# Narrow cross attention as one program per layer, with packed norm statistics and key and query units inside the batch loop

## The reference, cut to what matters

```python
y_dca, y_main = y[:, -DCA:, :], y[:, :-DCA, :]
kv_dca = (y_dca @ Wkv_dca + bkv_dca).reshape(b, DCA, 2, H, HD)
k_dca = _ln(kv_dca[:, :, 0], kn_dca_w, kn_dca_b);  v_dca = kv_dca[:, :, 1]
q = _ln((x @ Wq + bq).reshape(b, s1, H, HD), qn_w, qn_b)      # norm over 16 features
k = _ln(y_main @ Wk + bk, kn_w, kn_b);  v = y_main @ Wv + bv  # per head, as above
out = (softmax(q k / 4) v + softmax(q k_dca / 4) v_dca) @ Wo + bo
x = x + out                                                   # q is made of layernorm(x)
```

## Time and profile before

| what | us |
|---|---|
| median of 3 runs (lowest, highest) | 3232.19 (3231.69, 3232.72) |
| profiled execution, first to last instruction (the page gives no other time of it) | 3231.0 |
| L1 narrow cross attention, first instruction to the last addition to x | 238.7 |
| the same of L2 and of L3 | 238.2, 240.9 |

### The profile page before, as it was taken

How to read it: one execution, slowest core, us unless ns; L and a number is a source line. 1 busy time by engine, 2 the same in 40 slices (tenths; PEclk the granted TensorE clock), 3 DMA queues, 4 the chain that set the end, 5 groups by cost and what they waited for, 6 DMA issues and landing times. The chain is left out here.

```text
span 3231.0 us, 47747 instructions
## 1 busy us (share of the span) xinstructions
PE 2781.8 (86%) x17648; PEld 1732.3 (54%) x17648; DVE 1936.2 (60%) x2606; ACT 1423.1 (44%) x2574; POOL 917.8 (28%) x774
## 2 busy tenths in 40 slices
PE   7999986899997978789988875667989798998897
PEld 5998953466645647433345522223654455554686
DVE  3555545322268827444468779667965799994442
ACT  3333343121265536322265553446657666652123
POOL 0111100033104513000005400001530799990362
PEclk9999998899998989989998988878999899999898
DMA  4000004111200000200000000000000221213124
GB/s 154 1 0 0 0 7 154 64 46 45 68 29 2 2 21 2 82 1 0 0 20 2 11 4 0 0 20 1 2 28 14 78 77 67 77 44 107 50 87 145
DMA packets 72275, 122.16 MB, mean 38 GB/s; under 512 B 10720, under 2 KB 53088, under 8 KB 71584
## 3 DMA queue, kind: packets, MB, share of 16 engines
q1 hardware_dynamic: 63168, 95.25, 8.9%
q0 software_dynamic: 8928, 24.39, 2.5%
HBM read 100.88 MB, written 18.74 MB: 37 GB/s over the span
## 5 line engine op out<-in xcount | busy, mean ns | idle before, releaser
L3054 POOL TENSOR_TENSOR h<-ssm_u,ss_bc 128x1024 f32<-128x1024 f32 x88 | 205.6, 2358 | 0.0
L3017 ACT ACTIVATE ssm_p_h<-ss_delta,ss_decay 128x256 f32<-128x256 f32 x352 | 146.6, 463 | 123.6 <-DVE ctxT L3091 84.0
L2966 PE MATMUL ssm_p_y<-ctxT,ident 128*128 128x512 f32 x412 | 187.8, 596 | 0.0
L1375 POOL MEMSET ctxT<- 128x512 f32 x3 | 1.6, 526 | 602.8 <-POOLq L60 602.8
L639 POOL TENSOR_TENSOR xw_prob<-xw_prob,xw_rsum 128x512 f32<-128x512 f32 x64 | 65.8, 1039 | 361.1 <-DVE xw_rsum L620 361.1
L3086 DVE TENSOR_TENSOR_SCAN ssm_p_h<-ssm_p_h,h 128x1024 f32<-128x1024 f32 x64 | 145.8, 2279 | 8.5 <-ACT ssm_p_h L3017 6.8
L499 PEld LDWEIGHTS xw_p_q<-xw_u,xw_vo_h 128*128 128x128 f32 x1024 | 116.1, 192 | 10.7 <-ACT xw_u L569 10.2
L3044 POOL TENSOR_TENSOR ctxT<-ctxT,ss_bc 128x1024 f32<-128x1024 f32 x50 | 117.4, 2355 | 15.5 <-DVE ctxT L3084 15.5
L490 PEld LDWEIGHTS xw_p_q<-h,xw_m_h 128*128 128x128 f32 x1024 | 116.8, 192 | 8.9 <-issue 8.9
L2950 PE MATMUL ssm_p_h<-ssm_b_diagonal,ssm_uT 128*128 128x128 f32 x640 | 85.0, 289 | 40.6 <-DVE ctxT L3091 19.6
L2966 PEld LDWEIGHTS ssm_p_y<-ctxT,ident 128*128 128x128 f32 x412 | 76.5, 192 | 79.5 <-issue 78.3
(11 more groups left out here) (747 smaller groups left out, 7188.0 us busy)
## 6 DMA issues: line engine op xcount, KB each, us to landing
ss_bc<-ss_bc_rows SPq DMA_DIRECT2D x24, 896.0 KB, 4.4
ss_bc<-ss_bc_rows SPq DMA_DIRECT2D x8, 768.0 KB, 4.1
L3f_rows<-L3f_rows_out SPq DMA_DIRECT2D x16, 384.0 KB, 3.9
L0f_wg<-in_L_ffn_gate SPq DMA_DIRECT2D x9, 512.0 KB, 10.2
L0f_wu<-in_L_ffn_up SPq DMA_DIRECT2D x9, 512.0 KB, 9.9
L0f_wd<-in_L_ffn_down SPq DMA_DIRECT2D x9, 512.0 KB, 10.2
L0f_rows<-L0f_rows_out SPq DMA_DIRECT2D x16, 256.0 KB, 3.5
x<-in_xT SPq DMA_DIRECT2D x1, 2048.0 KB, 7.5
```

The lines of the kernel that those rows point to most:

```text
L2966: mm = pe.matmul(p_y[:, 2 * half:2 * half + 2, :].rearrange("p e t -> p (e t)"), k.ident[:, :], weighed[n % RING_W][:, ts(half, CH)], star ...
L3017: i = act.activation(out[:, ts(e, CT)], delta[:, e, ts(c, CT)], ACT.Exp, scale=decay[:, E4 * s + e:E4 * s + e + 1])
L3054: g.tensor_tensor(tiles(drive[n % RING]), u[:, c % 2, :, :], bcast(bcs[:, row_b(s), :], 1, E4), ALU.mult).then_inc(sem["driven_g"], 1)
```

## The change

Both programs become one, with one set of semaphores and no barrier. The 16 DCA tokens now lie first in each batch of the context (`SEG = ((DCA, S2), (0, DCA))`, rolled on the host), so `tails` (512 KB load) and the memset of `ctxT` go. The layer norm becomes `PackedNorm`: statistics of the four chunks in 4 x 32 partitions of one PSUM bank (one Ln and one Exp for all), spread again by matmuls into PSUM, where VectorE reads them. The 12 units come in the order `UNITS`; the first four (keys 0 to 2, query 0) are made ahead of the loop, the other eight (query 1, keys 3, 4, query 2, key 5, query 3, keys 6, 7) in the loop, in three pieces, in steps 3j-1, 3j and 3j+1 for j = 0 to 7: piece 0 is `project`, `add_bias` and `squares`; piece 1 is `tally` (head means into 4 x 32 partitions) and `inverse` (Ln and Exp of 128 elements per partition); piece 2 is `widen` (spread by a matmul that carries the norm weight), `multiply` on VectorE (reads PSUM) and `affine` on GpSimd (adds the shift). The squares move from VectorE to ScalarE. Projections and widened factors of the late units use the PSUM tile of the transposes (`p_tw`, `p_t`), the head means that of the values (`p_v`). `values` is one matmul of 512 columns and its copy two; `mix` of batch n-3 now stands ahead of `turn` of batch n-2; the output projection and the addition to x are for two batches each, every second step. The x addition t stands in VectorE's step 2t+5, after the reciprocal. `mix` waits for `added`, since it shares a bank with the output projection. All loops are unrolled. The kernel's start loads one matrix less (`head_mean`).

The diff, cut to what the argument uses ("..." marks what is left out):

```diff
+class PackedNorm:
...
+    def means(self, pe):
+        for a in range(H2):
+            for c in range(NCH):
+                mm = pe.matmul(self.p_stat[self.row(c), :], self.k.mean_ones[:, 0:32], self.src[:, a, ts(c, CH)], start=a == 0, stop=a == H2 - 1, skip_group_check=True)
+        mm.then_inc(self.sem["mean"], 1)
+
+    def copied(self, act):
+        act.wait_ge(self.sem["mean"], 1)
+        act.copy(self.stat[:, 0, :], self.p_stat).then_inc(self.sem["copied"], 1)
+
+    def spread(self, pe, pair):
+        pe.wait_ge(self.s_c, 16)
+        pe.wait_ge(self.sem["copied"], 1)
+        if pair == 1:
+            pe.wait_ge(self.sem["centred"], 2)
+        for c in (2 * pair, 2 * pair + 1):
+            mm = pe.matmul(self.p_wide[:, c % 2, :], self.pick[self.row(c), :], self.stat[self.row(c), 0, :], start=True, stop=True, skip_group_check=True)
+        mm.then_inc(self.sem["spread"], 1)
+
+    def centre(self, v, c):
+        v.wait_ge(self.sem["spread"], c // 2 + 1)
+        v.tensor_tensor(self.dst[:, :, ts(c, CH)], self.src[:, :, ts(c, CH)], bcast(self.p_wide[:, c % 2, :], 1, H2),
+                        ALU.subtract).then_inc(self.sem["centred"], 1)
+
...
+    SEG = ((DCA, S2), (0, DCA))
...
+    UNITS = ((KN, 0), (KN, 1), (KN, 2), (QN, 0), (QN, 1), (KN, 3), (KN, 4), (QN, 2), (KN, 5), (QN, 3), (KN, 6), (KN, 7))
+    EARLY, EVERY = 4, 3
...
+        p_sf = ps(k, ctx, "p_s", [P, 4, CH])
+        p_s = p_sf[:, :, 0:HALF].rearrange("p r (o s) -> p r o s", o=H2)
+        p_tw = ps(k, ctx, "p_t", [P, H2, CH])
+        p_t = p_tw[:, :, :].rearrange("p o (r q) -> p o r q", r=4)
+        p_v = ps(k, ctx, "p_v", [P, CH])
+        p_ys = ps(k, ctx, "p_y", [P, CH])
+        p_y = p_ys[:, 0:D].rearrange("p (o t) -> p o t", o=H2)
+        p_o = p_ys[:, D:D + P].rearrange("p (o t) -> p o t", o=H2)
+        p_c = p_ys[:, 0:3 * H2].rearrange("p (n o) -> p n o", n=3)
+        p_b = p_ys[:, P:P + 2 * H2].rearrange("p (o n) -> p o n", o=H2)
+        ln = PackedNorm(k, ctx, sem, k.x, k.h, p_v[:, :], p_tw, pick, s_c)
...
+        def front(i):
+
+            at = 2 * ((i + 1) % 2)
+            return p_sf[:, at:at + 2, :] if i < EARLY else p_tw
+
+        def variance(i):
+
+            return p_ys[:, 0:P] if i < EARLY else p_v[:, 0:P]
...
+        def at_step(n):
+
+            late = len(UNITS) - EARLY
+            return [(EARLY + j, n + 1 - EVERY * j) for j in range(late) if 0 <= n + 1 - EVERY * j < EVERY]
...
+            def turned_before(n):
+                if n >= 3:
+                    pe.wait_ge(sem["turned_read"], 2 * (n - 2))
+                else:
+                    pe.wait_ge(ln.sem["normed"], NCH)
...
+            def tally(i):
+                pe.wait_ge(s_h, 32)
+                pe.wait_ge(sem["squared"], i + 1)
+                if i >= 1:
+                    pe.wait_ge(sem["logged"], i)
...
+                for part in range(2):
+                    for j in range(4):
+                        at = 2 * P * (j % 2) + P * part
+                        mm = pe.matmul(variance(i)[32 * j:32 * j + 32, :], of_head[:, part, :], square[:, i % 2, j // 2, at:at + P], start=part == 0, stop=part == 1, skip_group_check=True)
+                mm.then_inc(sem["tallied"], 1)
+            def widen(i):
+                kind, _ = UNITS[i]
+                pe.wait_ge(sem["inverse"], i + 1)
+                for at in range(4):
+                    for m, (s0, s1) in kinds(kind):
+                        for o in range(H2):
+                            rows = slice(64 * o, 64 * o + 64)
+                            mm = pe.matmul(front(i)[:, o, at * P + s0:at * P + s1], heads[rows, m, at, :], rv[rows, i % 2, s0:s1], start=True, stop=True, skip_group_check=True)
+                mm.then_inc(sem["widened"], 1)
...
+            def values(n, tallied):
+                if n >= 1:
+                    pe.wait_ge(sem["v_copied"], n)
+                else:
+                    pe.wait_ge(ln.sem["rstd"], 1)
+                    pe.wait_ge(s_o, 32)
+                pe.wait_ge(sem["logged"], tallied)
+                pe.matmul(p_v[:, :], k.ctxT[:, ts(n, S2)], wv[:, :, :].rearrange("p n f -> p (n f)"), start=True, stop=True, skip_group_check=True).then_inc(sem["valued"], 1)
...
+            def mix(n):
+                pe.wait_ge(sem["v_copied"], n + 1)
                 if n >= 1:
-                    pe.wait_ge(sem["v_copied"], n)
+                    pe.wait_ge(sem["mixed_read"], n)
                 if n >= 2:
...
+            def step(n):
+                if 0 <= n < B - 1:
+                    score(n + 1)
+                units = at_step(n)
+                tallied = EARLY
+                for i, part in units:
+                    if part == 1:
+                        if n >= 3:
+                            pe.wait_ge(sem["v_copied"], n - 2)
+                        else:
+                            pe.wait_ge(ln.sem["rstd"], 1)
+                        tally(i)
+                    tallied = i + 1 if part >= 1 else i
+                if within(n, 2, B + 2):
+                    values(n - 2, min(tallied, len(UNITS)) if units else len(UNITS))
+                for i, part in units:
+                    if part == 0:
+                        turned_before(n)
+                        project(i)
+                    elif part == 2:
+                        turned_before(n)
+                        widen(i)
+                if n == -1:
+                    score(0)
+                if within(n, 3, B + 3):
+                    mix(n - 3)
+                if within(n, 2, B + 2):
+                    for i, part in units:
+                        if part == 0:
+                            pe.wait_ge(sem["biased"], i + 1)
+                        elif part == 2:
+                            pe.wait_ge(sem["scaled"], i + 1)
+                    turn(n - 2)
+                if n >= 4 and n % 2 == 0:
+                    project_out((n - 4) // 2)
+
+            ln.means(pe)
+            merge_keys()
+            merge()
+            ln.spread(pe, 0)
+            project(0)
+            ln.spread(pe, 1)
+            project(1)
+            ln.variances(pe, 0)
+            tally(0)
+            ln.variances(pe, 1)
+            widen(0)
+            merge_out()
+            tally(1)
+            ln.spread_inverse(pe, 0)
+            project(2)
+            widen(1)
+            ln.spread_inverse(pe, 1)
+            tally(2)
+            project(3)
+            widen(2)
+            tally(3)
...
+            def step(n):
+                units = at_step(n)
                 if within(n, 0, B):
                     act.wait_ge(sem["shifted"], n + 1)
-                    act.activation(prob[:, u, :, :, :], prob[:, u, :, :, :], ACT.Exp, scale=0.25).then_inc(sem["exped"], 1)
-                if within(n, 1, B + 1):
-                    act.wait_ge(sem["valued"], n)
-                    own = vx[:, (u + 1) % 2, :, :, :].rearrange("p o (r j) (s d) -> p (o r) (j s) d", j=2, s=2)[:, :, 0:4:3, :]
-                    act.copy(own, p_v.rearrange("p (g j d) -> p g j d", j=2, d=HD)).then_inc(sem["v_copied"], 1)
+                    act.activation(prob[:, n % 4, :, :, :], prob[:, n % 4, :, :, :], ACT.Exp, scale=0.25).then_inc(sem["exped"], 1)
+                for i, part in units:
+                    if part == 1:
+                        inverse(i)
                 if within(n, 2, B + 2):
+                    m = n - 2
+                    act.wait_ge(sem["valued"], m + 1)
+                    if m >= 2:
+                        act.wait_ge(sem["mixed"], m - 1)
+                    act.copy(own(m, slice(0, P)), p_v[:, 0:D].rearrange("p (g j d) -> p g j d", j=2, d=HD)).then_inc(sem["v_main"], 1)
+                    act.wait_ge(sem["v_main"], m + 1)
+                    act.copy(own(m, slice(0, DCA)), p_v[0:DCA, D:2 * D].rearrange("p (g j d) -> p g j d", j=2, d=HD)).then_inc(sem["v_copied"], 1)
+                for i, part in units:
+                    if part == 0:
+                        add_bias(i)
+                if within(n, 3, B + 3):
+                    m = n - 3
+                    act.wait_ge(sem["mixed"], m + 1)
+                    if m >= 4:
+                        act.wait_ge(sem["out_proj"], m // 2 - 1)
+                    act.copy(us[:, m // 2 % 2, :, ts(m % 2, S)], p_o).then_inc(sem["mixed_read"], 1)
+                if within(n, 2, B + 2):
+                    m = n - 2
                     for o in range(H2):
-                        act.wait_ge(sem["turned"], 2 * n + o - 3)
+                        act.wait_ge(sem["turned"], 2 * m + o + 1)
+                        if m >= 1:
+                            act.wait_ge(sem["mixed"], m)
                         act.copy(probT[:, o, :, :, :].rearrange("p r j t -> p (r j t)"), p_t[:, o, :, :].rearrange("p r q -> p (r q)")).then_inc(sem["turned_read"], 1)
-                    act.wait_ge(sem["mixed"], n - 1)
```

(123 more changed lines are left out.)

467 lines of the change are left out of this document (204 added, 263 removed).

## The result

The changed kernel takes 3364.86 us (median of 4 runs, 3361.26 to 3366.89) against 3232.11 (4 runs, 3231.69 to 3232.72) before: ratio 1.0407, 95% interval 1.0393 to 1.0421. The forecast was 3325, with 3190 to 3420 as its range: the sign is right, the cost is 133 us where 93 were forecast. The profiled execution's span is 3362.5, 131.5 more than the 3231.0 of before.

What follows compares the result with a forecast made beforehand. VectorE and TensorE bound the loop before; after the change, latency through in-order queues does. 22.6 us more a stage, 68 in three, plus 25 for the clock, makes 93 over the span of 3231.0: 3325 by the median, range 3190 to 3420.

Steps and rivals of the forecast that it cites:

- start to the scores of batch 3: Part of a stage up to batch 3's scores: 94.4 us before, 58.6 after, a gain of 35.8.
- unit stretch, without clock: Batch 3's scores to batch 24's, seven late units as serial chains of waits: 154.9 us, 7.4 a step.
- clock in it: TensorE's clock loss in the steps with units: 1.2 us a unit, 8 a stage, 25 in all.
- seven steps without a unit: Batches 24 to 31, VectorE at 4.03 plus 0.22 us a step: 4.25 each, 29.8 in all.
- after the scores of batch 31: End of a stage: 18.9 us before, one shorter projection at the end, so 18.0.
- stage: One whole narrow cross attention: 238.7 us before, 261.3 after, plus 8 for the clock.
- The rival of pieces that fit: In the loop, late units' pieces fit: some 15 us a unit, 3150 in all; chance 0.17.
- the signs that the forecast named: Unit steps: `multiply` waits near 5 us, `tally` above 1, scores 21 to 23 per three steps, VectorE idle a third.
- `widen` of keys: Spread of a key unit's factors on TensorE: 1.3 us at the scores' pace, taken; 4.2 at the merge's.
- the rival with the clock mostly at half: Clock falls for most unit steps: 5 to 9 us more a unit, 3390 to 3490 in all; chance 0.14.
- the 22.6: Forecast growth of one stage without clock loss, from 238.7 to 261.3 us; 68 in three stages.
- the two additions: VectorE's additions to x in front of multiply 3, ahead of the loop: 2.6 us, done at 39.3.

Runs made afterwards that it cites:

- e6: Changed kernel plus 512-column products nobody reads, on TensorE in its longest wait of each unit (three behind `widen` or two behind the output projection): 3320.69 us.
- e5: Changed kernel plus one VectorE sum over 896 elements per partition (1.09 us) per loop unit, directly ahead of `multiply`: 3363.14 us.
- e1: Changed kernel with `multiply` moved on VectorE behind the sums, the reciprocal and the addition to x of its step: 3293.68 us.
- e2: Changed kernel with ScalarE's order changed: squares ahead of the copies of the transposes, `inverse` ahead of Exp of the batch: 3320.98 us.
- e8: Kernel before with only its second program replaced by the new loop; norm and all twelve units stay in the first program: 3198.54 us, ratio 0.9891.
- e3: Changed kernel with the edits of e1 and e2 together: 3285.63 us.

## Why the prediction was right or wrong

| step of the prediction (us a stage) | forecast | measured |
|---|---|---|
| start to the scores of batch 3 | 58.6 | 68.4 |
| unit stretch, without clock | 154.9 | 155.2 (e6) |
| clock in it | 8 | 11.6 (e6) |
| seven steps without a unit | 29.8 | 29.1 |
| after the scores of batch 31 | 18.0 | 16.5 |
| stage | 269.3 | 280.8 |

**What bounds the loop.** Right. Latency through in-order queues, not busy time, sets the unit stretch: e5 adds work at no cost, e1 and e2 move work and gain 71 and 44. The rival of pieces that fit was to be recognised by unit steps under 6.2; they are 7.9 in the mean (166.8 / 21). Of the signs that the forecast named, these are in the trace: tally's wait for squares above 1 (1.23 in key units), VectorE idle for a third or more, `multiply` waiting for `widen` (6.8 in the mean of the five key units and 4.1 of the three query units, where near 5 was said), scores 4.2 apart after batch 24 where 4.3 was said. Two were missed: scores are 22.7 to 26.2 apart per three steps where 21 to 23 were said, three of the seven above 24, and batch 3's come at 68.4 where 55 to 65 were said.

**The unit stretch.** Right in its sum at full clock, 155.2 (e6) for 154.9, but in part because errors cancel: the first of the seven units, which still starts at half clock, takes 23.1 for 21.2, and five of the others less than was said. `widen` of keys takes 1.96, not 1.3: it lay between the bounds, and the scores' pace, from which 1.3 came, doesn't hold for the small products (16 columns) in it. `tally` takes 0.65, not 0.5. Against that, the three key units with a projection in their second step take 22.4 in e6 where the forecast had 22.7, and the two query units 21.8 where it had 22.2: the second step, with its projection, takes 6.7 (scores at 1036.54 and 1043.24) where the forecast's terms give 7.2. The wait of `mix` for the x addition (3.28) has no line in the forecast's timeline, though the change's text has it; it ran beside the path that had been priced, so that it cost no time at full clock (in e6 the scores behind it still wait 0.73 for VectorE). What it did cost is the clock behind it, and e1 shows how much hung on that place. `mix` and the output projection share a PSUM bank, and the Trainium skill, PSUM — Partial Sum Buffer, "PSUM bank collisions raise a hardware error", asks for semaphores by bank and quadrant, not by address. The kernel keeps to this, and the 3.28 is the wait that comes of it; no run here does without.

**The clock.** Right in kind, 8 forecast and 11.6 measured in the unit stretch; the rival with the clock mostly at half (5 to 9 a unit) is out, at 1.7 a unit. (That rival's own price, 35 to 63 a stage on top of the 22.6, makes 3405 to 3490; its lower end of 3390 was too low.)

**Ahead of batch 3's scores: the step that failed.** The forecast priced the part ahead at full clock throughout, 44.1 to the first scores and 58.6 to batch 3's. The first scores came at 52.6. PE's timeline there:

```profile
911.40 3.23 PE L1233 MATMUL L1x_p_v<-L1x_pn_square,mean_ones 128*32 128x512 f32 x8 [2.42 <-ACT L1x_pn_square L1226]
...
919.32 2.08 PE L1248 MATMUL L1x_p_t<-L1x_pn_stat,L1x_pick 32*128 32x512 f32 x4 [0.51 <-ACT L1x_pn_stat L1240]
921.33 4.10 PE L1409 MATMUL L1x_p_s<-ctxT,L1x_wkc 128*128 128x448 f32 x8
...
940.84 6.22 PE L1405 MATMUL L1x_p_t<-h,L1x_wqc 128*128 128x512 f32 x8 [3.09 <-issue]
```

The same instructions at full clock take 1.96 (`widen`), 1.13 (spread), 2.16 (a key projection, 904.54) and 3.70 (a query projection, 928.93). After a wait of 2.42 for ScalarE's squares and one of 3.09 they run at half clock: the granted clock is 0.71 from 912 to 920, 0.66 from 920 to 928 and 0.70 from 936 to 944, where before had 0.98 in the whole part. Spread, project and query projection lose 0.95 + 1.94 + 2.52 = 5.4. Three key `widen`, each 0.66 over their price, add 2.0. A third term is the additions to x in front of multiply 3:

```profile
935.71 3.90 DVE L1701 TENSOR_SCALAR x<-x,L1x_out_bias 128x2048 f32<-128x2048 f32 x2
```

The forecast had 2.6 for the two additions, and in the kernel before, where GpSimd does nothing meanwhile, they take 2.47 (at 951.15). Here GpSimd's affine (L1719, from 935.87) runs beside them: one addition takes 1.28 and the other 2.70, and the affine 3.99 where it takes 2.04 at 928.72. L2 and L3 show the same. The project of query 1 stands behind multiply 3, so this is on the path and costs 1.3. These three make 8.7, against a first score that is 8.5 late. From the first scores to batch 3's it is 15.8 where 14.5 was said, with one row of scores and a `widen` at half clock in it (1.24 and 2.08 for 0.73 and 1.16).

The forecast had put its loss of clock in the unit stretch alone, though it had named the mechanism itself: a wait of 3 us in TensorE's queue, then half clock. This stretch, 9.8 a stage or 29 in three, is most of the 40 by which the forecast fell short, and by these rows 6.8 of the 9.8 are half clock (5.4 and 1.4); no run took the clock loss out of this part alone. The clock in the unit stretch (3.6 a stage) is the next, and the shorter end and steps give 2.2 back.

**The rest of the loop.** Right and slightly too cautious: 29.1 for 29.8, 16.5 for 18.0. The forecast priced the new loop without units for 7 steps only. It did not ask what that loop gives over all 32 batches, which e8 answers: it is the part of the change that pays.

**What stays open.** e3's unit stretch of 142.65 shows a clock of 0.96, so that its 20.4 a unit is mostly the chain of waits. A chain with more banks couldn't be tried: all eight are taken (four for scores, two for transposes, one each for values and output). The 3 us outside the three stages of the changed kernel, and the 7 that e8's span (3197.9) gives back outside its own, lie in the other sublayers and are not explained.

## What to carry to other kernels

Before work is put into "free" engines of a pipelined loop, follow one item of it by hand through every in-order queue that it passes, with each tile that it shares: its latency, and not the idle time it fills, is the price, and here it was 10.6 us a unit in the loop (84.9 / 8) against 5.6 ahead of it (44.8 / 8). Where a wait must stand in a queue, put it behind everything there that doesn't depend on it: this one edit gave back half of the loss. When a change does several things, measure the part that shortens the loop without the part that fills it.

## What the runs showed that had not been expected

- Products that nobody reads make the kernel faster by 44 us (e6): five 512-column products a pair of units, at 0.95 each, against a clock of 0.89 in the unit stretch.
- Eight 512-column products onto 32 outputs take 1.92 in all where the same columns onto 128 outputs take 0.93 each (3.70 for four): placed in different quarters of the outputs they run side by side, nearly four at a time. The forecast had left open 6.9 for them in single file.
- Sixteen `widen` products of 64 rows take 1.96 and eight take 1.16: those of 16 columns cost 0.10 each, hardly less than the 0.14 of those with 112 or 128.
- Two additions on VectorE to x on VectorE take 3.90 beside GpSimd's affine, which itself takes 3.99 for its usual 2.04, and 2.47 where GpSimd is idle (kernel before). Work put on GpSimd wasn't free there.
